# Second attention: key and query slots with four rows per group, returned as one transfer of 128 partitions

## The chip, the core and the metric

The kernel runs on one NeuronCore of a Trainium2 chip. The metric is the device time of one execution in microseconds (us); lower is better. The profile names the engines PE (TensorE), DVE (VectorE), ACT (ScalarE), POOL (GpSimd) and SP (SyncE, which here only issues transfers). SBUF is the on-chip memory of 128 partitions, PSUM holds the results of PE in eight banks.

## The reference, cut to what matters

Four layers over 1024 tokens of 512 numbers, each followed by a residual sum and a layer norm: a small attention across heads, a ternary feed-forward, a windowed causal attention with rotary positions ("the second attention"), and a mixture of experts. The change touches only the second attention:

```python
q = q * cos + rotate_half(q) * sin
k = k * cos + rotate_half(k) * sin
scores = einsum('bhqd,bhkd->bhqk', q, k) / sqrt(16)
allowed = (j <= i) & (j > i - 128)
attn = softmax(where(allowed, scores, -inf))
out = einsum('bhqk,bhkd->bhqd', attn, v) @ Wo.T
```

It has 32 heads of 16 numbers, and each block of 128 query tokens sees its own block of keys and the one before.

## The kernel before, in words

The second attention works on 8 tiles t of 128 tokens. For each tile PE multiplies by the key, query and value weights (`project2`), DVE rotates keys and queries (`rotate`, `rope_sum`), PE turns them so that head dimensions lie along partitions (`turn_rotated`). To keep float32 accuracy from products in a shorter format, each tensor is kept as a high part (ACT, `parts_out_high`) and a low part (DVE, `parts_low`). A product of two such tensors needs three terms: high by high, low by high, high by low.

The three terms are folded into one product by stacking rows. A head has 16 dimensions, and for each of them the stack holds three rows: for keys high, high, low and for queries high, low, high. So a head fills 48 rows. Two heads share the 128 partitions, one from partition 0 and one from partition 64 (`KS` = 64). The stack is built by a detour through device memory (the scratch tensor `ys`, called `slots_out` in the profile):

- SP (`relay_rows`, line 866) writes three blocks of 256 KB for each tensor of each tile. The group of a dimension has 3 rows in device memory, and each write fills one of them.
- POOL (`stack_rows`, line 1803) waits for the three writes and issues two transfers of 384 KB that bring the 96 rows back: 48 rows to partitions 0 to 47, 48 rows to partitions 64 to 111, each row 8 KB. Keys go to `kS` (a part of tile `RP`), four slots in rotation; queries go to `qS` (`XR` or `QS`), three slots in rotation.

Scores are computed twice. `row_scores` (line 573) multiplies queries by keys over 48 rows, and DVE takes the row maxima from it (`row_maxima`, line 1185). The maxima are split, turned, and written by POOL (`stack_maxima`, line 1810, four transfers of 8 KB per tile) as two more rows, 48 and 49 of each half, of `qS`. The matching rows of `kS` hold minus one: POOL sets whole key slots to minus one before first use (`minus_ready`, lines 1792, 1830 and 1838). `key_scores` (line 586) then multiplies keys by queries over 50 rows, which gives scores with the maximum subtracted; ACT exponentiates (`weights_out`), POOL masks (`mask`, lines 1818 and 1821), PE weighs the values (`weigh`, line 601).

One loop, written out by hand in the same form for each engine, sets the order: `for i in range(-1, T)` with eight steps. In turn i the engines do row scores of tile i + 1, key scores of tile i, projections and relay of tile i + 2, and output of tile i - 1. Each engine works through its own list in order. In turn i POOL issues the return of the keys of tile i + 2 in step 4 and of its queries in step 5, then the first maxima of tile i + 1 in step 6. PE needs the returned tile at the first `row_scores` of the next turn, and the maxima at the first `key_scores` behind that. All POOL transfers share one queue (q0). After the last tile's blocks are written, SP issues loads of shared expert weights (768 KB each), a gate matrix and a table.

Of the kernel before, what the change touches and what calls it, by code (L numbers as in the profile page):

```python
# [5 lines left out]
F32 = mybir.dt.float32  # L6
F32R = mybir.dt.float32r
# [8 lines left out]
P = 128  # L16
# [5 lines left out]
HD = D // H  # L22
KS = 64
# [56 lines left out]
def build(nc, x, wq, wk, wv, bias, k0, k1, k2, s0, s1, s2, aq, ak, av, ao, gate, experts, shared,  # L80
          rope_c, factor_c, table_c, out, xs, ys):
    with ExitStack() as ctx:
        def sb(name, shape, dt):
            return ctx.enter_context(nc.sbuf_tensor(name, shape, dt))

        def sem(name):
            return ctx.enter_context(nc.semaphore(name))
# [32 lines left out]
        slots = sb("slots", [P, TOP, T], U32)  # L120
# [5 lines left out]
        with nc.sbuf_tensor("QS", [P, 18432], F32R) as QS:  # L126
# [27 lines left out]
        qS = [t.rearrange("p (a q) -> p a q", q=P) for t in (XR[:, 2048:4096], QS[:, 0:2048], QS[:, 2048:4096])]  # L154
        kS = RP[:, :].rearrange("p (s a k) -> p s a k", s=4, k=P)
# [12 lines left out]
        XT2 = XR[:, 0:2048].rearrange("p (b a c n) -> p b a c n", b=2, a=2, c=DC)  # L168
        x2T = [QS[:, 0:1024].rearrange("p (a c n) -> p a c n", a=2, c=DC)] + [XT2[:, 0]] * (T - 1)
        coT = XT2[:, 1]  # L170
        relay_in = [[ys[a:a + 3 * P, :].bitcast(F32R).rearrange("(d m) n -> d (m n)", m=4) for a in (6 * P * n, 6 * P * n + 3 * P)]
                    for n in range(2)]
        relay = [[ys[a:a + 3 * P, :].rearrange("(x b m) n -> b x m n", b=3, m=4) for a in (6 * P * n, 6 * P * n + 3 * P)]
                 for n in range(2)]

        wblock = [FP[:, c:c + WCOLS] for c in (14336, 14336 + WCOLS, 0, WCOLS, 8704, 8704 + WCOLS)]
        xblock = FP[:, 3072:5120].rearrange("p (b n) -> p b n", b=XB_)
# [85 lines left out]
        parts_out = [sem("qparts_out"), sem("kparts_out")]  # L263
        stack_in = [[sem(f"qstack_in{b}") for b in range(2)], [sem(f"kstack_in{b}") for b in range(2)]]
        max_in = [sem(f"max_in{f}") for f in range(2)]
        minus_ready = sem("minus_ready")
        diag_zero = sem("diag_zero")
        kdiag_in = [sem(f"kdiag_in{n}") for n in range(5)]
        kq_split = sem("kq_split")
# [31 lines left out]
        def window(i):  # L301

            cur, prev = i % 4, (i - 1) % 4
            if i == 0:
                return cur, 0
            if prev < cur:
                return slice(prev, cur + 1, cur - prev), P
            return slice(cur, prev + 1, prev - cur), 0
# [6 lines left out]
        def parts(t, n):  # L315

            return parts_k if n == 1 else parts_q[0 if t < 2 else 1]
# [10 lines left out]
        def _(pe):  # L328
# [171 lines left out]
            def half(hh, rows):  # L500

                return slice(KS * hh, KS * hh + rows)
# [59 lines left out]
            def row_scores(i, s):  # L562

                if s == 0:
                    pe.wait_ge(stack_in[1][i % 2], 32 * (i // 2 + 1))
                    pe.wait_ge(stack_in[0][i % 2], 32 * (i // 2 + 1))
                slots, _ = window(i)
                n = P if i == 0 else 2 * P
                both = [V.fill(pe, ("rowscores", i, 2 * s + a))[:, :].rearrange("p (a k) -> p a k", a=2)[:, :, 0:n] for a in range(2)]
                for m in range(2):  # L570
                    pr = 2 * s + m
                    for a in range(2):
                        mm = nc.tensor.matmul(both[a][:, m, :], qS[i % 3][half(a, 3 * HD), pr, :], kS[half(a, 3 * HD), slots, pr, :],  # L573
                                              start=True, stop=True)
                        if m == 1:
                            mm.then_inc(V.full, 1)

            def key_scores(i, hg, w):

                if w == 0 and hg % 4 == 0:  # L580
                    pe.wait_ge(max_in[hg // 4], 32 * (i + 1))
                both = [Q.fill(pe, ("keyscores", i, hg + a, w)) for a in range(2)]
                for m in range(4):
                    pr = 4 * (hg // 2) + m
                    for a in range(2):
                        mm = nc.tensor.matmul(both[a][:, m * P:(m + 1) * P], kS[half(a, 3 * HD + 2), (i - w) % 4, pr, :],  # L586
                                              qS[i % 3][half(a, 3 * HD + 2), pr, :], start=True, stop=True)
                        if m == 3:
                            mm.then_inc(Q.full, 1)

# [44 lines left out]
            for i in range(-1, T):  # L635
                t, r, d = i + 2, i + 1, i - 1
                for s in range(8):
                    if r < T:
                        row_scores(r, s)
                    if i >= 0 and (s % 2 == 0 or i >= 1):  # L640
                        key_scores(i, 2 * (s // 2), s % 2)
# [63 lines left out]
            b = V.fill(pe, "logits")  # L705
            for t in range(T):
                mm = nc.tensor.transpose(b[:, t * E:(t + 1) * E], lgT[:, t * P:(t + 1) * P], ident[0:E, 0:E])
# [52 lines left out]
            for k in range(len(ITEMS)):  # L760
# [6 lines left out]
                if k == 0:  # L767

                    pe.wait_ge(picked_ready, 2)
                    b = V.fill(pe, "ranks")[:, 0:(T + 1) * E]  # L770
                    nc.tensor.matmul(b, before[:, :], picked[:, :, :], start=True, stop=False)
                    for t in range(T):
                        nc.tensor.matmul(b[:, (t + 1) * E:(T + 1) * E], onesb[:, :], picked[:, t:t + 1, :].broadcast_to([P, T - t, E]),
                                         start=False, stop=False)
# [8 lines left out]
            for t in range(G, T):  # L783
                pe.wait_ge(tile_gathered[t], 16 * TOP)
                pe.wait_ge(diagonals_ready, TOP * G)
                for k in range(TOP):
                    mm = nc.tensor.matmul(acc[t - G][:, :], diagonal[:, TOP * (t - G) + k, :], gathered[:, (TOP * t + k) % YG, :],
                                          start=False, stop=(k == TOP - 1))
# [4 lines left out]
        def _(sp):  # L793
# [29 lines left out]
            def load_raw(n, w):  # L823
                sp.dma_start(raw_c[n].rearrange("p (c n) -> p c n", c=DC), w.rearrange("(c p) n -> p c n", p=P)).then_inc(wc_in[n], 16)
# [3 lines left out]
            for k in range(2 * NCH):  # L828
# [12 lines left out]
                for j in range(G):  # L841
                    rows = slice(32 * j, 32 * j + HD)
# [13 lines left out]
            def relay_rows(t, n):  # L856

                m = 2 * t + 1 - n
                if t >= 2:
                    sp.wait_ge(stack_in[n][t % 2], 32 * (t // 2))  # L860
                for blk, l in ((0, 0), (1 + n, 0), (2 - n, 1)):
                    if l == 0:
                        sp.wait_ge(parts_high, m + 1)
                    else:
                        U.drained(sp, ("turned", t, n))
                    sp.dma_start(relay[n][t % 2][blk], parts(t, n)[:, l, :].bitcast(F32)).then_inc(parts_out[n], 16)

            for t in range(T):
                relay_rows(t, 1)
                relay_rows(t, 0)  # L870
                if t == 1:
                    A.filled(sp, ("hidden", 1, 1, DC - 1))
                    sp.wait_ge(stack_in[0][1], 32)
                    load_raw(3, ao)
            sp.wait_ge(rotated, 2 * T)
            sp.wait_ge(parts_out[0], 48 * T)
# [850 lines left out]
        def _(p):  # L1727
# [14 lines left out]
            for k, (base, step) in enumerate(((0, -1), (-1, 1), (0, -1))):  # L1742
                m = maskb[:, k * P:(k + 1) * P]
# [45 lines left out]
            A.filled(p, ("hidden", 0, 1, DC - 1))  # L1789
            nc.gpsimd.memset(vaug[:, :, :, HD:HD + 1], 1.0).then_inc(ones_ready, 1)  # L1790
            for n in range(2):
                nc.gpsimd.memset(kS[:, n].bitcast(F32), -1.0).then_inc(minus_ready, 1)
            def stack_rows(t, n):

                p.wait_ge(parts_out[n], 48 * (t + 1))
                if t >= 3:
                    Q.filled(p, ("keyscores", t - 3, 7, 1 if t >= 4 else 0))
                if n == 1:
                    p.wait_ge(minus_ready, min(t, 3) + 1)
                rows = relay_in[n][t % 2]  # L1800
                for a in range(2):
                    dst = (qS[t % 3], kS[:, t % 4])[n][KS * a:KS * a + 3 * HD]
                    nc.gpsimd.dma_start(dst.rearrange("d a q -> d (a q)"), rows[3 * HD * a:3 * HD * a + 3 * HD]).then_inc(stack_in[n][t % 2], 16)

            def stack_maxima(t, f):

                U.drained(p, ("mx", t, f))
                for a in range(2):
                    place = KS * a + 3 * HD
                    nc.gpsimd.dma_start(qS[t % 3][place:place + 2, 8 * f:8 * f + 8, :],  # L1810
                                        mxT[HD * a:HD * a + HD, f, :]).then_inc(max_in[f], 16)

            def mask(i, hg, w):
# [10 lines left out]

            stack_rows(0, 1)
            stack_rows(0, 0)
            stack_rows(1, 1)
            stack_rows(1, 0)
            A.filled(p, ("ffn", T - 1))
            nc.gpsimd.memset(kS[:, 2].bitcast(F32), -1.0).then_inc(minus_ready, 1)  # L1830
            for i in range(-1, T):
                t, r = i + 2, i + 1
                for step in range(8):
                    if (i, step) == (1, 0):
                        p.wait_ge(w_high, 16)
                        nc.gpsimd.tensor_tensor(W[:, 7, :], raw_c[3], W[:, 6, :].bitcast(F32), ALU.subtract).then_inc(wo_split, 1)
                    if (i, step) == (0, 3):
                        nc.gpsimd.memset(kS[:, 3].bitcast(F32), -1.0).then_inc(minus_ready, 1)
                    if i >= 0 and (step % 2 == 0 or i >= 1):
                        mask(i, 2 * (step // 2), step % 2)  # L1840
                    if step == 2 and i >= 0:
                        stack_maxima(i, 1)
                    if step == 4 and 2 <= t < T:
                        stack_rows(t, 1)
                    if step == 5 and 2 <= t < T:
                        stack_rows(t, 0)
                    if step == 6 and r < T:
                        stack_maxima(r, 0)
# [76 lines left out]
```

## Time and profile before

| | |
|---|---|
| median of 3 runs | 733.93 us (730.81 to 736.4) |
| profiled execution | 731.17 us |
| its span, first to last instruction | 729.4 us |
| busy: PE / DVE / ACT / POOL | 615.2 / 393.2 / 270.8 / 239.0 us |
| mean granted TensorE clock | 0.918 of 2.4 GHz |
| turns i = 0 to 7 of the second attention | about 250 to 511 us |

Device time is a little longer than the span, since starting and ending the program lie outside it. Busy times overlap; what counts is which engine or transfer the others wait for at a given place. In a row of the timeline the bracket at the end is the idle time of the engine before the row and what released it; "issue" there means that the profile shows no releaser.

### The profile page before, as it was taken

To read this page: it belongs to the slowest core of one execution; us is meant where nothing else is said; L and a number is where in the kernel's file an instruction comes from. 1 tells how busy PE (TensorE), PEld (TensorE's weight loads), DVE (VectorE), ACT (ScalarE), POOL (GpSimd) and SP (SyncE) were. 2 spreads that over 40 slices of the span, in tenths; PEclk is the share of its full clock that TensorE was granted. 3 is DMA by queue.
4 is the path that set the end of the run, shared out by engine and by line. 5 is a ranking of instruction groups with operands and counts; after the bars stand their busy time and mean duration, and the time that the engine had idled before them with its cause. 6 is when DMAs were issued, how large, how long until landed. Compare 5 with 4: busy or idle time off the path is not lost.

```text
span 729.4 us, 13453 instructions
## 1 busy us (share of the span) xinstructions
PE 615.2 (84%) x5108; PEld 485.6 (67%) x5108; DVE 393.2 (54%) x1126; ACT 270.8 (37%) x433; POOL 239.0 (33%) x348
## 2 busy tenths in 40 slices
PE   2998999669889787998979896868789699999985
PEld 2987977557667565666757664645558588888762
DVE  4315445697765775767666684552464133323355
ACT  5155036366563323424243442444530112221313
POOL 6002523543310245535343552462007311111072
PEclk9999999999999886999898997577899899999998
DMA  8921211442057444618171638020007759997455
GB/s 304 392 103 27 54 34 25 104 134 74 0 145 155 106 116 61 155 23 176 35 143 46 131 110 165 2 89 3 0 1 283 279 178 409 415 418 286 185 167 193
DMA packets 49455, 104.37 MB, mean 143 GB/s; under 512 B 12208, under 2 KB 18480, under 8 KB 47856
## 3 DMA queue, kind: packets, MB, share of 16 engines
q1 hardware_dynamic: 30032, 61.68, 24.0%
q0 software_dynamic: 13744, 31.61, 18.9%
q10 hardware_dynamic: 5616, 10.23, 3.9%
q8 instruction: 41, 0.67, 0.4%
q14 instruction: 22, 0.18, 0.1%
HBM read 63.77 MB, written 35.13 MB: 136 GB/s over the span
## 4 chain that ended last, share of the span: by engine, by line
PE 53%; DMA 13%; DVE 10%; ACT 9%; issue 8%; POOL 6%; SPq 1%; POOLq 0%; ACTq 0%; DVEq 0%
PE bank L332 12%; PE bank L515 11%; PE bank L368 9%; DMA slots_out<-FP 5%; ACT FP L1451 4%; DVE FP L915 4%; PE bank L601 3%; PE bank L586 3%; PE bank L573 3%; POOL slots_in L1854 2%; POOL FP L1866 2%; DMA QS<-QS 2%; PE bank L391 2%; PE bank L546 2%; PE bank L379 1%
## 5 line engine op out<-in xcount | busy, mean ns | idle before, releaser
L1451 ACT ACTIVATE FP<-bank 128x512 f32<-128x512 f32 (+1 forms) x244 | 138.7, 611 | 316.3 <-PE bank L586 131.1
L1185 DVE CUSTOM_DVE_ANT_0 kraw<-bank,maskb 128x256 bf16<-128x256 f32 (+1 forms) x256 | 88.5, 401 | 60.1 <-PE bank L573 60.1
L515 PE MATMUL bank<-W,XR 128*128 128x512 f32 x348 | 107.0, 454 | 0.1
L332 PE MATMUL bank<-FP 128*128 128x128 f32 x558 | 89.1, 315 | 1.0 <-ACT FP L1451 1.0
L515 PEld LDWEIGHTS bank<-W,XR 128*128 128x128 f32 x348 | 72.0, 219 | 16.3 <-DVE XR L915 0.3
L368 PE MATMUL bank<-W,XR 128*128 128x512 f32 x288 | 77.6, 419 | 5.2 <-DVE W L915 5.2
L1818 POOL TENSOR_SCALAR_AFFINE_SELECT FP<-FP 128x512 f32<-128x512 f32 x64 | 41.4, 670 | 112.4 <-ACT FP L1451 112.4
L368 PEld LDWEIGHTS bank<-W,XR 128*128 128x128 f32 x288 | 64.2, 271 | 11.8 <-DVE W L915 5.6
L332 PEld LDWEIGHTS bank<-FP 128*128 128x128 f32 x558 | 66.9, 196 | 3.0 <-DVE FP L915 1.6
L915 DVE TENSOR_TENSOR FP<-FP,bank 128x128 f32<-128x128 f32 (+1 forms) x39 | 14.4, 370 | 68.4 <-ACT FP L1451 47.4
L332 PE MATMUL bank<-RP,W 128*128 128x512 f32 x192 | 45.8, 394 | 2.2 <-DVE FP L915 2.2
L1821 POOL TENSOR_SCALAR_AFFINE_SELECT FP<-FP 128x512 f32<-128x512 f32 x56 | 38.0, 705 | 29.3 <-ACT FP L1451 29.1
L1859 POOL DMA_DIRECT2D FP<-slots_in x31 | 16.7, 540 | 86.5 <-PE bank L717 79.9
L1774 POOL DMA_DIRECT2D RPF<-FP x64 | 31.5, 502 | 38.5 <-PE bank L404 27.8
L332 PEld LDWEIGHTS bank<-RP,W 128*128 128x128 f32 x192 | 35.7, 188 | 10.5 <-issue 1.8
L573 PE MATMUL bank<-RP,QS 48*128 48x256 f32 x160 | 23.7, 377 | 22.6 <-issue 11.8
L1386 DVE COPY FP<-bank 128x512 f32<-128x512 f32 x31 | 21.4, 691 | 37.4 <-PE bank L717 37.4
L601 PE MATMUL bank<-FP 128*17 128x128 f32 x960 | 37.9, 308 | 2.0 <-ACT FP L1451 1.8
L915 DVE TENSOR_TENSOR XR<-bank,XR 128x512 fp32r<-128x512 f32 x27 | 21.3, 806 | 31.6 <-ACT XR L1451 31.6
L573 PEld LDWEIGHTS bank<-RP,QS 48*128 48x128 f32 x160 | 14.7, 222 | 34.0 <-issue 24.4
L601 PEld LDWEIGHTS bank<-FP 128*17 128x17 f32 x960 | 26.6, 108 | 13.1 <-issue 6.0
L1854 POOL DMA_INDIRECT slots_in<-X,slots x16 | 16.7, 1045 | 48.1 <-issue 48.1
(168 smaller groups left out, 1019.4 us busy)
## 6 DMA issues: line engine op xcount, KB each, us to landing
FP<-in_experts_dram SPq DMA_DIRECT2D x31, 768.0 KB, 9.6
slots_out<-QS SPq DMA_DIRECT2D x48, 256.0 KB, 2.8
FP<-slots_in POOLq DMA_DIRECT2D x31, 256.0 KB, 6.5
slots_out<-FP ACTq DMA_DIRECT2D x31, 256.0 KB, 8.0
slots_in<-RP SPq DMA_DIRECT2D x7, 1024.0 KB, 13.6
RP<-slots_out POOLq DMA_DIRECT2D x16, 384.0 KB, 6.0
QS<-slots_out POOLq DMA_DIRECT2D x10, 384.0 KB, 8.3
FP<-in_shared_dram SPq DMA_DIRECT2D x4, 768.0 KB, 7.6
```

The lines of the kernel that those rows point to most:

```text
L332: mm = nc.tensor.matmul(bank, lhs, rhs, start=(n == 0), stop=(n == len(terms) - 1))
L368: mm = nc.tensor.matmul(b[:, :], *terms[m], start=(m == 0), stop=(m == 3 * DC - 1))
L515: mm = nc.tensor.matmul(b[:, :], *terms[n], start=(n == 0), stop=(n == len(terms) - 1))
L573: mm = nc.tensor.matmul(both[a][:, m, :], qS[i % 3][half(a, 3 * HD), pr, :], kS[half(a, 3 * HD), slots, pr, :], start=True, stop=True)
L601: mm = nc.tensor.matmul(weighing[32 * q:32 * q + HD + 1, (h // 4 % 4) * P:(h // 4 % 4 + 1) * P], vaug[:, (i - w) % 4, head(h), :], PT[hg % ...
L915: return nc.vector.tensor_tensor(o, a, b, op)
L1185: ins = nc.vector.tensor_tensor_reduce(masked[:, 2 * (f % 2) + m, 0:n], b[:, m, :], maskb[:, m0:m0 + n], 1.0, -BIG, ALU.add, ALU.max, hmax ...
L1451: return nc.scalar.activation(o, i, func, **kw)
L1774: nc.gpsimd.dma_start(vdiag[k % 3][32 * g:32 * g + 32, 272 * g:272 * g + 272].rearrange("p (s d) -> p s d", s=CH), vT[32 * g:32 * g + 32, ...
L1818: ins = nc.gpsimd.affine_select(out=pt, in_=pt, compare_op=ALU.is_ge, fill=0.0, base=0, pattern=[[0, 4], [1, P]], channel_multiplier=-1)
L1821: ins = nc.gpsimd.affine_select(out=pt, in_=pt, compare_op=ALU.is_ge, fill=0.0, base=-1, pattern=[[0, 4], [-1, P]], channel_multiplier=1)
L1854: nc.gpsimd.indirect_dma_start(xs, bass.IndirectOffsetOnAxis(slots[:, k, t:t + 1], 0), X[:, t, :], None).then_inc(scattered, 16)
```

## The change

The group of a dimension has four rows instead of three, in device memory and in SBUF. The fourth row holds minus ones for keys and zeros for queries. These are written once, into both buffers of each tensor, by four transfers of 256 KB that SP issues ahead of the first relay (`edge_in`), from two memsets of 32 partitions (`edge_ready`). A returned tensor is now 128 rows of 8 KB, brought by one transfer to all 128 partitions. The maxima overwrite rows 3 and 7 of each half of the query slot. `row_scores` and `key_scores` run over 64 rows. The memsets of whole key slots, the wait for them in `stack_rows`, and one of the two transfers per tensor are gone; counts of 32 become 16.

```diff
-        relay_in = [[ys[a:a + 3 * P, :].bitcast(F32R).rearrange("(d m) n -> d (m n)", m=4) for a in (6 * P * n, 6 * P * n + 3 * P)]
+        places = [[slice(4 * P * (2 * n + b), 4 * P * (2 * n + b + 1)) for b in range(2)] for n in range(2)]
+        relay_in = [[ys[rows, :].bitcast(F32R).rearrange("(d m) n -> d (m n)", m=4) for rows in of] for of in places]
...
-                        mm = nc.tensor.matmul(both[a][:, m, :], qS[i % 3][half(a, 3 * HD), pr, :], kS[half(a, 3 * HD), slots, pr, :],
+                        mm = nc.tensor.matmul(both[a][:, m, :], qS[i % 3][half(a, KS), pr, :], kS[half(a, KS), slots, pr, :],
...
-                        mm = nc.tensor.matmul(both[a][:, m * P:(m + 1) * P], kS[half(a, 3 * HD + 2), (i - w) % 4, pr, :],
-                                              qS[i % 3][half(a, 3 * HD + 2), pr, :], start=True, stop=True)
+                        mm = nc.tensor.matmul(both[a][:, m * P:(m + 1) * P], kS[half(a, KS), (i - w) % 4, pr, :],
+                                              qS[i % 3][half(a, KS), pr, :], start=True, stop=True)
...
+            for n in range(2):
+                sp.wait_ge(edge_ready, n + 1)
+                for b in range(2):
+                    sp.dma_start(relay[1 - n][b][3].rearrange("x m n -> x (m n)"),
+                                 kS[0:P // 4, n].rearrange("p a k -> p (a k)").bitcast(F32)).then_inc(edge_in, 16)
...
-                nc.gpsimd.memset(kS[:, n].bitcast(F32), -1.0).then_inc(minus_ready, 1)
+                nc.gpsimd.memset(kS[0:P // 4, n].bitcast(F32), (-1.0, 0.0)[n]).then_inc(edge_ready, 1)
...
-                if n == 1:
-                    p.wait_ge(minus_ready, min(t, 3) + 1)
-                rows = relay_in[n][t % 2]
-                for a in range(2):
-                    dst = (qS[t % 3], kS[:, t % 4])[n][KS * a:KS * a + 3 * HD]
-                    nc.gpsimd.dma_start(dst.rearrange("d a q -> d (a q)"), rows[3 * HD * a:3 * HD * a + 3 * HD]).then_inc(stack_in[n][t % 2], 16)
+                if t == 0:
+                    p.wait_ge(edge_in, 64)
+                dst = (qS[t % 3], kS[:, t % 4])[n]
+                nc.gpsimd.dma_start(dst.rearrange("d a q -> d (a q)"), relay_in[n][t % 2]).then_inc(stack_in[n][t % 2], 16)
...
-                    place = KS * a + 3 * HD
-                    nc.gpsimd.dma_start(qS[t % 3][place:place + 2, 8 * f:8 * f + 8, :],
+                    nc.gpsimd.dma_start(qS[t % 3][KS * a + 3:KS * a + 8:4, 8 * f:8 * f + 8, :],
...
-            nc.gpsimd.memset(kS[:, 2].bitcast(F32), -1.0).then_inc(minus_ready, 1)
...
-                    if (i, step) == (0, 3):
-                        nc.gpsimd.memset(kS[:, 3].bitcast(F32), -1.0).then_inc(minus_ready, 1)
```

## Rows read from the trace of the kernel before

**Rows 1.** The page's chain that ended last, shares of the span by engine.

```profile
PE 53%; DMA 13%; DVE 10%; ACT 9%; issue 8%; POOL 6%; SPq 1%; POOLq 0%; ACTq 0%; DVEq 0%
```

**Rows 2.** Windows: length, busy us of five engines, clock share, transfer share, GB/s.

```profile
347.10:380.70 33.60, 29.71 (x300) 22.92 (x300) 22.40 (x91) 12.48 (x23) 14.74 (x24) 0.90 0.45 96
452.90:481.00 28.10, 25.79 (x262) 19.67 (x262) 18.70 (x81) 13.53 (x23) 11.91 (x20) 0.63 0.02 2
```

**Rows 3.** Timeline of PE, first score products of turns 1 to 6.

```profile
281.81 0.80 PE L573 MATMUL bank<-RP,QS 48*128 48x256 f32 x4 [2.86 <-DMA QS<-slots_out]
...
314.11 0.50 PE L573 MATMUL bank<-RP,XR 48*128 48x256 f32 x4 [0.99 <-issue]
315.25 0.66 PE L586 MATMUL bank<-QS,RP 50*128 50x128 f32 x8 [0.64 <-DMA QS<-QS]
...
347.08 0.56 PE L573 MATMUL bank<-RP,QS 48*128 48x256 f32 x4 [2.52 <-issue]
...
380.69 0.50 PE L573 MATMUL bank<-RP,QS 48*128 48x256 f32 x4 [2.36 <-issue]
381.89 0.47 PE L586 MATMUL bank<-QS,RP 50*128 50x128 f32 x2 [0.69 <-DMA QS<-QS]
...
414.91 0.50 PE L573 MATMUL bank<-RP,XR 48*128 48x256 f32 x4 [2.34 <-issue]
...
452.93 0.80 PE L573 MATMUL bank<-RP,QS 48*128 48x256 f32 x4 [6.94 <-issue]
```

**Rows 4.** Timeline of POOL: transfer issues of turn 2, and of turn 5.

```profile
335.27 1.07 POOL L1803 DMA_DIRECT2D RP<-slots_out  x2
...
337.52 1.05 POOL L1803 DMA_DIRECT2D QS<-slots_out  x2
...
435.14 1.07 POOL L1803 DMA_DIRECT2D RP<-slots_out  x2
```

**Rows 5.** Transfer issues within 338.1:338.2 and 341.7:341.8, KB, us to landing.

```profile
QS<-slots_out POOLq DMA_DIRECT2D x1, 384.0 KB, 8.9
...
XR<-QS POOLq DMA_DIRECT2D x1, 8.0 KB, 6.0
```

**Rows 6.** All 32 transfers of line 1810, issue to landing.

```profile
DMA to landing us min/median/max: 1.8/3.1/10.2
```

**Rows 7.** Windows: a return alone; then expert loads. Last column GB/s.

```profile
336.50:345.50 9.00, 8.05 (x136) 5.98 (x134) 6.23 (x27) 3.92 (x8) 5.65 (x10) 1.00 1.15 178
600.00:609.00 9.00, 9.00 (x65) 7.18 (x65) 4.03 (x8) 2.62 (x6) 1.61 (x3) 1.00 1.01 379
```

**Rows 8.** Transfer issues, 430 to 456 us.

```profile
FP<-in_shared_dram SPq DMA_DIRECT2D x2, 768.0 KB, 13.3
...
QS<-slots_out POOLq DMA_DIRECT2D x2, 384.0 KB, 12.9
```

**Rows 9.** Timeline of DVE behind the end of turn 2.

```profile
345.22 0.18 DVE L943 BATCH_NORM_AGGREGATE mv<-st 128x2 f32<-128x6 f32 x1
```

**Rows 10.** Timeline of PE: the two projections of turn 3.

```profile
349.45 5.21 PE L515 MATMUL bank<-W,XR 128*128 128x512 f32 x12
...
355.84 2.99 PE L515 MATMUL bank<-W,XR 128*128 128x512 f32 x12
```

**Rows 11.** Windows of half granted clock in turns 3 and 6.

```profile
347.40:354.20 6.80, 6.80 (x27) 5.47 (x24) 2.21 (x11) 1.09 (x2) 1.22 (x2) 0.50 0.00 0
449.80:473.70 23.90, 18.81 (x158) 14.59 (x160) 12.43 (x59) 9.66 (x15) 8.39 (x14) 0.50 0.12 17
```

**Rows 12.** Instructions by form: weight loads, least, median, longest ns.

```profile
L573 PEld LDWEIGHTS bank<-RP,QS x160: 182/186/335, 250.5 to 475.6; 48*128 48x128 f32 x160
...
L332 PEld LDWEIGHTS bank<-RP,W x192: 186/188/192, 534.5 to 703.4; 128*128 128x128 f32 x192
```

**Rows 13.** Timeline of POOL: the first return, and a memset.

```profile
206.89 1.02 POOL L1803 DMA_DIRECT2D RP<-slots_out  x2 [16.93 <-DMA slots_out<-QS]
...
245.35 1.80 POOL L1830 MEMSET RP<- 128x2048 f32 x1 [5.67 <-PE bank L332]
```

More of the change, by code:

```diff
@@ L170, in build @@
         coT = XT2[:, 1]
-        relay_in = [[ys[a:a + 3 * P, :].bitcast(F32R).rearrange("(d m) n -> d (m n)", m=4) for a in (6 * P * n, 6 * P * n + 3 * P)]
-                    for n in range(2)]
-        relay = [[ys[a:a + 3 * P, :].rearrange("(x b m) n -> b x m n", b=3, m=4) for a in (6 * P * n, 6 * P * n + 3 * P)]
-                 for n in range(2)]
+        places = [[slice(4 * P * (2 * n + b), 4 * P * (2 * n + b + 1)) for b in range(2)] for n in range(2)]
+        relay_in = [[ys[rows, :].bitcast(F32R).rearrange("(d m) n -> d (m n)", m=4) for rows in of] for of in places]
+        relay = [[ys[rows, :].rearrange("(x b m) n -> b x m n", b=4, m=4) for rows in of] for of in places]
         wblock = [FP[:, c:c + WCOLS] for c in (14336, 14336 + WCOLS, 0, WCOLS, 8704, 8704 + WCOLS)]
@@ L265, in build @@
         max_in = [sem(f"max_in{f}") for f in range(2)]
-        minus_ready = sem("minus_ready")
+        edge_ready = sem("edge_ready")
+        edge_in = sem("edge_in")
         diag_zero = sem("diag_zero")
@@ L564, in row_scores @@
                 if s == 0:
-                    pe.wait_ge(stack_in[1][i % 2], 32 * (i // 2 + 1))
-                    pe.wait_ge(stack_in[0][i % 2], 32 * (i // 2 + 1))
+                    pe.wait_ge(stack_in[1][i % 2], 16 * (i // 2 + 1))
+                    pe.wait_ge(stack_in[0][i % 2], 16 * (i // 2 + 1))
                 slots, _ = window(i)
@@ L859, in relay_rows @@
                 if t >= 2:
-                    sp.wait_ge(stack_in[n][t % 2], 32 * (t // 2))
+                    sp.wait_ge(stack_in[n][t % 2], 16 * (t // 2))
                 for blk, l in ((0, 0), (1 + n, 0), (2 - n, 1)):
@@ L872, in _ @@
                     A.filled(sp, ("hidden", 1, 1, DC - 1))
-                    sp.wait_ge(stack_in[0][1], 32)
+                    sp.wait_ge(stack_in[0][1], 16)
                     load_raw(3, ao)
```

## The prediction

> **What bounds the kernel now.** I read the views in this order: the page's chain, the second attention cut into its turns, the waits of PE at the turn boundaries, the transfers that end those waits, and the clock.
>
> The chain is PE for 53% of the span and transfers for 13% [rows 1]; some of its "issue" share is transfers too, as will be seen. In a middle turn PE is busy 29.71 of 33.60 us, DVE 22.40, POOL 14.74, ACT 12.48 [rows 2]. PE is the bound there, so a microsecond in which PE stands still in a turn is one lost, and the other engines have room. The long stops of PE all sit at the same place, the first row scores of a new turn: 2.86, 0.99, 2.52, 2.36, 2.34 and 6.94 us in turns 1 to 6, and twice the first key scores behind them, 0.64 and 0.69 us [rows 3]. Together 19.34 us.
>
> Who ends them? In turn 1 the profile names the returned queries, elsewhere it says "issue". The landings settle it. For the tile that turn 3 needs, POOL issues the keys from 335.27 and the queries from 337.52 [rows 4]. The second half of the queries, issued near 338.1, takes 8.9 us, so it lands at 347.0; PE starts at 347.08 [rows 3, 5]. The first maxima stand behind it on POOL's queue: near 341.7 they need 6.0 us, where the quickest of that line needs 1.8 [rows 5, 6]. So the return ends the wait at each boundary, and it delays the maxima as well.
>
> **Part 1: the return is one transfer of 128 partitions.** The fixed part of a POOL transfer I take as 1.8 us, the quickest landing of an 8 KB one [rows 6]. From the issue of the keys to the landing of the queries are 11.7 us (335.27 to 347.0), of which 9.9 us carry four times 384 KB, 1.57 MB: 159 GB/s. A window laid over it shows 178 GB/s with the transfer engines busy throughout (share over 1), while expert loads to all 128 partitions, with stores and other loads beside them, run at 379 GB/s with a share of 1.01 [rows 7]. So the engines here are not short of work but slow at it: each transfer writes into only 48 partitions.
>
> The new return brings 2.10 MB in two transfers. At 379 GB/s that is 5.5 us; with 1.8 us it lands at 342.6, at 159 GB/s it is 13.2 us and lands at 350.3. These are the ends. I take 379, because the width of the destination is what sets the two rows apart. PE is free at 344.56 (347.08 less 2.52). Any rate above 2.10 MB in 7.5 us, 280 GB/s, hides the return wholly; below 212 GB/s (2.10 MB in 9.9 us) it is later than now.
>
> The Trainium skill, "SBUF — State Buffer", section "Door 1: The DMA port swizzle", says that a transfer's rate follows from how many of 16 ports its partitions reach, that partitions 0 to 63 reach only 8, and that two transfers on the two halves, issued together, hardly gain on one. The rows with 48 partitions agree in direction. By its 328 GB/s for 1 MiB on 128 partitions, an estimate, the return would land at 343.5, still hidden.
>
> What is late next at a boundary? DVE's last work of turn 2 ends at 345.40, 0.84 us after PE is free [rows 9], but that is the layer norm's statistics; PE's two banks for row scores were emptied before it. The maxima, issued near 341.7 behind the queries, land by 343.5 with 1.8 us. So in turns 2 to 5 I count the stops wholly: 0.99 + 0.64 + 2.52 + 2.36 + 0.69 + 2.34 = 9.54 us. In turn 1 the last return issue is later against PE, and 2.86 us are gained if it is 2.86 us earlier; 4.4 us (9.9 less 5.5) are at hand, so 2.86.
>
> Turn 6 is different: the shared loads of 1.57 MB run beside the return, both land after about 13 us [rows 8]. Return and shared loads are 3.67 MB; at 379 GB/s from the keys' issue at 435.14 [rows 4], with 1.8 us, all is in at 446.6, where PE is free at 445.99 [rows 3]. The keys are ahead of the shared loads, the queries among them. I take a rest of 0.9 us, with ends of 0 and 3, so 6.0 us are gained. Sum of part 1: 9.54 + 2.86 + 6.0 = 18.4 us.
>
> **Part 2: the clock.** Behind a stop at a boundary PE often runs at half clock. In turn 3 the granted clock is 0.50 from 347.4 to 354.2 [rows 11], that is 1.2 of 2.4 GHz, after the idle 2.52 us; twelve products take 5.21 us in it and 2.99 us after it [rows 10]. So a half-clocked us of PE work gives back 1 - 2.99/5.21 = 0.43 us. Like stretches follow the other stops in turns 2 to 5, at most 6.8 us each. Three times 6.8 us, 20.4 us, would give 8.8 us as an upper end; the lower end is 0, since a fall can also have another cause. I take 5 us. Turn 6 runs at half clock until 473.7 [rows 11], 20.8 us of it, which would be 8.9 us; but the turn has few large products, and DVE with 18.70 us of work in 28.10 [rows 2] soon becomes the bound. I take 1 us there and 1 us in turn 1, ends 0 and 6. Sum: 7 us.
>
> The stops could go without their clock; then the gain is 18.4 us alone.
>
> **Part 3: longer products.** Four products of 256 columns over 48 rows take 0.50 us [rows 3], that is 1024 columns; twelve of 512 over 128 rows take 2.99 us, which is also 0.50 us for 1024 [rows 10]. Weight loads take 186 ns at 48 rows and 188 at 128 [rows 12]. Rows are free; 0.
>
> **Part 4: the edge rows.** Two memsets stay, with fewer partitions; two of 1.80 us go, one of them ahead of the first maxima of turn 0, where PE next waits for DVE, so 0 gained [rows 13]. SP issues four more transfers of 256 KB while it would wait anyway: the first return waits 16.93 us for its blocks and is issued at 206.89 [rows 13], and is needed over 20 us later. Cost 0; if that cover were gone, four issues and the transfers, some 5 us. The added wait for `edge_in` stands ahead of the first return only, where nothing else is queued that PE needs.
>
> **Part 5: one POOL issue less per tensor.** Half of 1.07 us each [rows 4] falls away. The queries are issued about 0.5 us sooner; this is margin, 0.
>
> **Sum.** 18.4 + 7 = 25.4 us. The profiled execution took 731.17 us, so 705.8; it lay 2.8 us under the median 733.93. Against the median: 708.5, said as 708.
>
> **Rivals.**
>
> A, the price goes by bytes (slower). If the return is slow for another reason than the 48 partitions, say reads of scratch rows in device memory, 2.10 MB at 159 GB/s need 13.2 us instead of 9.9: 3.3 us more at each of six boundaries, 20 us, and the clock stays as it is: 754. The place is PE's wait at each turn's first row scores, and it decides from 212 GB/s down. For it: POOL's queue shows no fast large transfer alone in these rows. Against: 379 GB/s with POOL's own block loads in it [rows 7]. The Trainium skill, "DMA: Bandwidth & Descriptors", section "Anatomy of one DMA", has a fit by bytes alone, 2.0 us plus bytes over 436 GB/s: an estimate of 2.9 us for 384 KB and 4.4 us for 1 MB, one transfer for two of which would gain next to nothing. Its 2.9 us stand against 8.9 us in the trace.
>
> B, stops go, another wait comes. The rotation on DVE, the exponentials on ACT or the maxima's way become late once PE is ahead, and the clock still falls, as half clock is also seen where PE never waited for a return. Then half to two thirds of 18.4 us are gained: 9 to 12, which gives 722 to 725.
>
> C, nothing measurable: the stop is ended by something that only coincides with the landing. Then 734. The landing at 347.0 and the start at 347.08 speak against it.
>
> **How the numbers follow.** Forecast, stops gone and part of the clock back: 0.75, 700 to 717. B: 0.13. A: 0.05. C: 0.03. More than that, with turn 6 at full clock (19.3 + 8.8 + 7 = 35, so 699 or less): 0.04. The upper end of the range takes in part of B, stops gone by two thirds and no clock: 722. The lower end is 698. No change is within 1% (7 us), about what a measurement here can tell; A is the slower case, with a little for a clock that gets worse: faster 0.91, same 0.04, slower 0.05.
>
> **What would show it.** Right: returned tensors of 1 MB land within 5 to 6 us of issue; the stops of PE at the first row scores are under 0.5 us in turns 1 to 5 and under 3 in turn 6; the maxima land in about 2 us; a middle turn lasts 28 to 31 us instead of 33.6. Wrong: landings of 7 us or more, rate in the return under 212 GB/s; or fast landings with new idle time of PE before turned or weighed tiles; or half-clock stretches that stay though the stops are gone.

## The result and the profile after

The changed kernel takes 707.76 us (median of 4 runs, 702.0 to 710.99) against 732.37 us before (4 runs): a ratio of 0.9649 with a 95% interval of 0.9569 to 0.973. The profiled execution took 710.99 us, its span is 709.3 us, at a mean granted clock of 0.926. It is the slowest of the four runs, so its span tells a little less than the medians: 20.1 us less than before, where the medians differ by 24.6.

The page's chain, to set beside [rows 1]: transfers fall from 13% to 6%, PE rises from 53% to 60%.

```profile
PE 60%; DVE 11%; ACT 9%; issue 6%; DMA 6%; POOL 5%; SPq 1%; POOLq 0%; ACTq 0%; DVEq 0%
```

The timeline of PE at the same first products as [rows 3]; a turn without a bracket began without a stop:

```profile
279.78 0.80 PE L573 MATMUL bank<-RP,QS 64*128 64x256 f32 x4 [0.75 <-DVE hmax L1190]
...
309.83 0.50 PE L573 MATMUL bank<-RP,XR 64*128 64x256 f32 x4 [0.58 <-issue]
311.40 0.66 PE L586 MATMUL bank<-QS,RP 64*128 64x128 f32 x8 [1.06 <-DMA QS<-QS]
...
340.53 0.50 PE L573 MATMUL bank<-RP,QS 64*128 64x256 f32 x4
...
368.86 0.51 PE L573 MATMUL bank<-RP,QS 64*128 64x256 f32 x4 [0.41 <-issue]
...
396.76 0.50 PE L573 MATMUL bank<-RP,XR 64*128 64x256 f32 x4
...
427.30 0.80 PE L573 MATMUL bank<-RP,QS 64*128 64x256 f32 x4 [2.62 <-issue]
428.83 1.11 PE L586 MATMUL bank<-XR,RP 64*128 64x128 f32 x8 [0.73 <-DMA XR<-QS]
```

The stops add up to 6.15 us where there were 19.34. Ahead of turns 3 and 5 there is none. Turn 0 now ends on the row maxima of DVE, a new releaser in place of the returned queries, and over half of what is left (2.62 and 0.73 us) stands before turn 6, where the shared loads run beside the return.

The transfer that stood at 335.27 and 337.52 before is issued at 329.78 and 331.90 now. Each is one transfer; size in KB and us from issue to landing (windows 329.9:330 and 332.1:332.2):

```profile
RP<-slots_out POOLq DMA_DIRECT2D x1, 1024.0 KB, 5.3
```

```profile
QS<-slots_out POOLq DMA_DIRECT2D x1, 1024.0 KB, 7.0
```

So the queries land at 338.9, 9.1 us after the keys' issue (11.7 before), and PE comes for them at 340.53: 1.6 us of margin.

Windows: the first two answer to [rows 2], the middle one to the return in [rows 7], the last two to [rows 11].

```profile
340.50:368.90 28.40, 26.44 (x304) 20.51 (x300) 22.71 (x93) 12.89 (x24) 13.76 (x22) 1.00 0.39 133
427.30:455.70 28.40, 25.52 (x252) 19.24 (x252) 17.48 (x79) 12.32 (x20) 11.90 (x20) 0.59 0.02 4
...
331.00:338.60 7.60, 7.60 (x75) 5.18 (x73) 3.51 (x18) 3.29 (x7) 4.17 (x8) 0.78 0.83 279
...
426.50:450.40 23.90, 20.40 (x167) 15.63 (x167) 13.21 (x64) 9.65 (x15) 8.39 (x14) 0.50 0.04 10
460.60:484.50 23.90, 20.80 (x167) 14.49 (x168) 3.52 (x10) 8.77 (x15) 9.60 (x17) 0.50 0.15 53
```

Turn 3 lasts 28.4 us, 5.2 less than before, at full clock throughout. The window begins behind the stop ahead of turn 3, so of these 5.2 us only 2.0 are a stop, the one at its end ahead of turn 4 (2.36 us, now 0.41). The rest is work: PE is busy for 26.44 us in it where it needed 29.71, with the same products, at the other clock. Turn 6 is the exception. It is 28.4 us long and was 26.7 (452.93 to the first product of turn 7 at 479.63), and about 23 us of it, from its start to 450.4, are at half clock.

### The profile page after: what moved, and what is told of

Same layout as the page of the kernel before. It is cut to its first block, busy times and chain, and to the rows that moved or that the text cites. A ratio compares the mean times of both kernels' runs of the same rounds, so it can differ in the third digit from the quotient of the medians.

```text
span 709.3 us, 13439 instructions
## 1 busy us (share of the span) xinstructions
PE 607.8 (86%) x5108; PEld 479.8 (68%) x5108; DVE 393.1 (55%) x1126; ACT 270.8 (38%) x433; POOL 228.3 (32%) x330
## 3 DMA queue, kind: packets, MB, share of 16 engines
q1 hardware_dynamic: 30224, 62.73, 24.6%
## 4 chain that ended last, share of the span: by engine, by line
PE 60%; DVE 11%; ACT 9%; issue 6%; DMA 6%; POOL 5%; SPq 1%; POOLq 0%; ACTq 0%; DVEq 0%
PE bank L332 17%; PE bank L515 11%; PE bank L368 9%; ACT FP L1456 4%; DVE FP L920 4%; PE bank L601 4%; PE bank L586 3%; PE bank L573 3%; POOL slots_in L1853 2%; PE bank L717 2%; POOL FP L1865 2%; DVE kraw L1190 2%; PE bank L391 2%; PE bank L379 1%; PE bank L546 1%
## 5 line engine op out<-in xcount | busy, mean ns | idle before, releaser
L515 PE MATMUL bank<-W,XR 128*128 128x512 f32 x348 | 99.8, 429 | 0.1
L368 PE MATMUL bank<-W,XR 128*128 128x512 f32 x288 | 76.3, 414 | 5.2 <-DVE W L920 5.2
L515 PEld LDWEIGHTS bank<-W,XR 128*128 128x128 f32 x348 | 66.5, 202 | 14.6 <-DVE XR L920 0.3
L368 PEld LDWEIGHTS bank<-W,XR 128*128 128x128 f32 x288 | 63.6, 270 | 11.1 <-DVE W L920 5.6
L1823 POOL TENSOR_SCALAR_AFFINE_SELECT FP<-FP 128x512 f32<-128x512 f32 x56 | 37.9, 701 | 23.6 <-ACT FP L1456 23.3
L920 DVE TENSOR_TENSOR XR<-bank,XR 128x512 fp32r<-128x512 f32 x27 | 21.3, 807 | 31.9 <-ACT XR L1456 31.9
L601 PEld LDWEIGHTS bank<-FP 128*17 128x17 f32 x960 | 26.6, 108 | 13.2 <-issue 5.7
L573 PE MATMUL bank<-RP,QS 64*128 64x256 f32 x160 | 23.7, 378 | 11.5 <-DVE hmax L1190 8.5
L717 PEld LDWEIGHTS bank<-ident,FP 128*128 128x128 f32 x124 | 15.7, 144 | 21.5 <-issue 15.7
```

The source lines that it names most:

```text
L368: mm = nc.tensor.matmul(b[:, :], *terms[m], start=(m == 0), stop=(m == 3 * DC - 1))
L515: mm = nc.tensor.matmul(b[:, :], *terms[n], start=(n == 0), stop=(n == len(terms) - 1))
L573: mm = nc.tensor.matmul(both[a][:, m, :], qS[i % 3][half(a, KS), pr, :], kS[half(a, KS), slots, pr, :], start=True, stop=True)
L601: mm = nc.tensor.matmul(weighing[32 * q:32 * q + HD + 1, (h // 4 % 4) * P:(h // 4 % 4 + 1) * P], vaug[:, (i - w) % 4, head(h), :], PT[hg % ...
L920: return nc.vector.tensor_tensor(o, a, b, op)
L1823: ins = nc.gpsimd.affine_select(out=pt, in_=pt, compare_op=ALU.is_ge, fill=0.0, base=-1, pattern=[[0, 4], [-1, P]], channel_multiplier=1)
```

## Experiments

The kernel before was timed again beside each group of kernels: median 734.0 us beside two halves, two combs, the later loads in the changed kernel and the first kernel with idle products in turn 6; 729.9 us beside the others. So kernels of different groups are compared by their ratios to the kernel before, not by their medians.

**Two halves, and two combs.** Both keep the four-row layout, its bytes and the new loads of 64 rows; only the return is cut in two.

```diff
-                nc.gpsimd.dma_start(dst.rearrange("d a q -> d (a q)"), relay_in[n][t % 2]).then_inc(stack_in[n][t % 2], 16)
+                for a in range(2):
+                    nc.gpsimd.dma_start(dst[KS * a:KS * a + KS].rearrange("d a q -> d (a q)"), relay_in[n][t % 2][KS * a:KS * a + KS])\
+                        .then_inc(stack_in[n][t % 2], 16)
```

The combs differ in the slices alone: `dst[a:P:2]` and `relay_in[n][t % 2][a:P:2]`.

> The changed kernel, but each tensor returns in two transfers of 512 KB, one to partitions 0 to 63 and one to partitions 64 to 127; same bytes, same rows, same products. Theory (the rate follows from how widely one transfer spreads over the partitions): the return is slow again. Before, 1.57 MB in four such transfers took 9.9 us behind a fixed 1.8 us; now 2.10 MB take between 9.9 and 13.2 us, so keys' issue to queries' landing is 11.7 to 15 us against 9.1 us in the changed kernel, the stops of PE at the first row scores come back with 2.5 to 5 us each, and the time is 728 to 752 us. Rival (one transfer fewer per tensor is what helps, or bytes alone count): one more issue of 0.53 us per tensor and nothing else, 707 to 713 us.

> The changed kernel, but each tensor returns in two transfers of 512 KB, one to the even and one to the odd partitions. Theory (spread over the partitions): both transfers reach as far as one of 128 partitions, so the return takes 9 to 10 us as in the changed kernel, and the time is 705 to 713 us. Rival (the single transfer is what helps): as slow as with two halves, 728 us or more. Neither kernel changes the number of bytes.

Measured: two halves 735.95 us (10 runs), a ratio of 1.0069 to the kernel before (1.0024 to 1.0114); two combs 704.52 us (4 runs), 0.9666 (0.9596 to 0.9735). Windows over one return, first of the kernel with halves, then of the one with combs (last column GB/s):

```profile
340.00:350.00 10.00, 9.56 (x136) 6.74 (x134) 5.81 (x26) 3.64 (x8) 5.60 (x10) 0.83 1.10 210
```

```profile
331.30:338.00 6.70, 6.70 (x96) 5.09 (x98) 4.16 (x21) 3.32 (x7) 5.52 (x10) 1.00 0.95 318
```

Issue to landing of all their returns of line 1807, halves and then combs:

```profile
DMA to landing us min/median/max: 4.9/7.3/15.6
```

```profile
DMA to landing us min/median/max: 3.8/4.9/10.3
```

From the issue of turn 3's keys to the landing of its queries are 12.9 us with halves (338.73 to 351.60) and 8.6 with combs (330.08 to 338.70). The transfer engines are about as busy in the one as in the other (1.10 and 0.95) and move 210 and 318 GB/s. Same bytes, same number of transfers, same queue: what differs is which partitions one transfer reaches. With halves the stops are back (4.30, 2.90, 2.13, 3.84, 3.32 and 9.20 us before turns 1 to 6), and the layout with more bytes is a small loss, 0.2 to 1.1%. This settles the spread of a transfer against rival A (bytes) and against "one transfer instead of two": the single transfer is not what helps. One thing moves along with the partitions: row d of the scratch tensor always goes to partition d, so a comb also reads every other row of device memory and a half reads adjacent ones. No run parts the two; that it is the side of the partitions is argued, not shown. The Trainium skill, "SBUF — State Buffer", section "Door 1: The DMA port swizzle", gives partition bits 2 to 4 and 6 as the choice of port; even and odd partitions alone reach every port by it. The combs agree, at 318 GB/s against 210. The same page says that only one transfer over all 128 partitions can reach all of them ("Can I just issue two DMAs to hit both halves?"); two combs of 64 partitions, which bring a tensor pair back as fast as two transfers over all 128 or faster (8.6 us against 9.1), are against that sentence.

**Stops filled with idle products, in the kernel before.** The products are extra work and change no result.

```diff
+                    if s == 0 and 1 <= i <= 6:
+                        fill_in((0, 12, 4, 10, 9, 9, 28)[i])     # products of 512 columns into a free bank
```

> The kernel before, with its slow return, but with idle products of 512 columns on PE ahead of the first row scores of turns 1 to 6 (12, 4, 10, 9, 9 and 28 of them), about as long as the stops of PE there and no longer. The stops keep their length but PE is busy in them. This measures the clock's part alone. Theory (the half-clock stretches behind the stops come from the stops): the stretches near 316, 347, 381, 415 and 450 us go, and 5 to 12 us are gained with no transfer made faster: 722 to 729 us. Rival (the stretches fall by chance or for other reasons): they stay and the time is 733 to 740 us.

Measured: 725.52 us (10 runs), 0.9952 of the kernel before (0.991 to 0.9995). Its timeline of PE ahead of turn 3, and the windows of turns 2 and 3:

```profile
344.76 2.25 PE L639 MATMUL bank<-W 128*128 128x512 f32 x9
347.86 0.51 PE L573 MATMUL bank<-RP,QS 48*128 48x256 f32 x4 [0.85 <-issue]
```

```profile
316.10:347.90 31.80, 29.16 (x310) 22.32 (x310) 22.40 (x91) 12.49 (x23) 14.74 (x24) 1.00 0.50 102
347.90:379.80 31.90, 28.88 (x309) 22.11 (x309) 22.39 (x91) 12.48 (x23) 14.73 (x24) 1.00 0.50 101
```

The trace has nine of the ten products issued there. PE comes to the row scores about as late as before, but works while it waits, and turns 2 and 3 stay at 2.4 GHz; turn 3 takes 31.9 us instead of 33.6. Turns 2 to 5 together take 131.9 us instead of 138.8. So the clock is a second price of a stop, and it is separable: 6.9 us in this profile for turns 2 to 5. Not all reaches the end: the twelve products ahead of turn 1 outlast the stop (turn 0 and its end take 33.9 us instead of 31.3). Turn 6 is still at half clock for 17.1 us, though 6.65 us of products stand in its stop and only 1.19 and 0.33 us of idle time are left:

```profile
451.40:468.50 17.10, 15.13 (x136) 11.45 (x136) 9.69 (x47) 8.57 (x13) 7.24 (x13) 0.50 0.02 3
```

The interval leaves 0.4 to 6.6 us for the whole, under 1%, where 5 to 12 was expected; the stretches behind the stops go as the theory said, up to turn 5, but the time gained, 3.5 us by the ratio, is less.

**Shared loads issued after the last return.** In the changed kernel, and in the kernel before.

```diff
             sp.wait_ge(parts_out[0], 48 * T)
+            sp.wait_ge(stack_in[0][1], 16 * (T // 2))            # 32 in the kernel before
             load_shared(0)
```

> The changed kernel, but SP waits for the landing of the last returned queries before it issues the first load of shared expert weights. Theory (the rest of the stop before turn 6, 2.62 and 0.73 us, comes from the shared loads on the same transfer engines): the queries land 7 us after issue instead of 9.7, the stop before turn 6 falls under 0.8 us, and 2.5 to 3.4 us are gained; the shared weights land about 6 us later and ACT needs the first of them some 6 us into turn 6, so 0 to 3 us of this may be lost. If the clock of turn 6 hangs on that stop, the half-clock stretch from 426 to 450 us goes too, for up to 6 us more: 699 to 706 us. Rival (the clock of turn 6 is low because the turn has few large products): the stop goes but the stretch stays, 704 to 708 us.

> The kernel before, but SP waits for the landing of the last returned queries before it issues the first load of shared expert weights. In the kernel before those loads land about 13 us after issue together with the queries. Theory (the stop of 6.94 us before turn 6 is the slow return plus the collision): the queries land 8 to 9 us after issue instead of 13, the stop before turn 6 becomes 2 to 3 us, and 4 to 5 us are gained, 728 to 731 us. Rival (the stop is the narrow return alone): no gain, 733 us.

Measured: 699.11 us (4 runs), 0.9593 of the kernel before (0.9522 to 0.9665); in the kernel before 726.99 us (10 runs), 0.9971 (0.9927 to 1.0016), which is not told from no change. Transfers of the first of these, 411 to 440 us, and its timeline and window at the start and over the length of turn 6:

```profile
FP<-in_shared_dram SPq DMA_DIRECT2D x2, 768.0 KB, 5.0
QS<-slots_out POOLq DMA_DIRECT2D x1, 1024.0 KB, 7.1
```

```profile
423.70 0.50 PE L573 MATMUL bank<-RP,QS 64*128 64x256 f32 x4
```

```profile
423.70:447.00 23.30, 19.38 (x254) 14.87 (x252) 17.78 (x81) 13.01 (x21) 11.91 (x20) 0.85 0.24 79
```

The queries land 7.1 us after issue where they took 9.7 beside the loads, and turn 6 starts without a stop. The loads themselves land in 5.0 us instead of 10.6 (medians of two), so waiting costs them little: they are in at 427.9 and 429.95 us, where the changed kernel had them at 425.5 and 428.4. Turn 6 then takes 23.3 us at a mean clock of 0.85 instead of 28.4 at 0.59. My rival, that the half-clock stretch stays when the stop goes, falls: it shrinks from 23.9 to 6.8 us. But the stop is not the whole cause. The 6.8 us that stay begin at 429.8, 6 us into a turn that began without a stop, and in the kernel before with filled stops turn 6 was at half clock for 17.1 us. What else lowers the clock in this turn is not shown. In the kernel before, the same wait cuts the stop ahead of turn 6 from 6.94 to 2.06 us, as expected, but turn 6 still begins with a stop and is at half clock for 17 us; the 4 to 5 us that this should have gained are not told from nothing in the time.

By its ratio the changed kernel with the later loads is the fastest that ran, level with the two kernels built on it below. Its four runs, 698.1 to 700.54 us, all lie below the changed kernel's four, 702.0 to 710.99; by the ratios, 0.9593 and 0.9649, the gain over the changed kernel is 4 us, by the medians 8.7, and the intervals of the ratios overlap. The gain is seen in the trace, in the stop and in turn 6; its size is open.

**Idle products in turns 6 and 7.** In the changed kernel (8 and then 3 per step of turn 6), and with the later loads (2 per step of turn 6, 4 of turn 7).

```diff
+                    if i in (6,) and s < 5:
+                        fill_in(8 if s == 0 else 3)
```

> The changed kernel with idle products on PE: 8 products of 512 columns ahead of the first row scores of turn 6 and 3 more ahead of each of its steps 1 to 4, 20 in all, from weights into a bank that nobody reads before it is overwritten. They add about 20 x 0.23 = 4.6 us of PE work at 2.4 GHz or 8 at 1.2 GHz; the first eight fall into the stop of 2.6 us. Theory (turns with few large products run at half clock, and PE is their bound only for that reason): the granted clock stays 1 through most of turn 6, its 28.4 us become 24 to 27, and the time is 703 to 708 us. Rival (the clock doesn't follow from PE's work here, or DVE and ACT bound the turn anyway): the turn grows by 2 to 6 us, 709 to 714 us.

> The changed kernel with the shared loads issued after the last return, and with idle products on PE: 2 of 512 columns ahead of each of the first five steps of turn 6, 4 ahead of each of the first five of turn 7. If a busy PE holds the full clock where nothing else is wrong, turns 6 and 7 run mostly at 2.4 GHz and up to 5 us are gained on the 699 us of the kernel with the later loads: 694 to 700 us. If turn 7 is bound by the chain through ACT, POOL and PE in turn, not by PE's clock, it is 699 to 703 us.

Measured: 704.67 us, 0.9655 (0.9581 to 0.9728), and 699.39 us, 0.9602 (0.9554 to 0.965). The window of turn 6 in the first:

```profile
426.30:454.30 28.00, 23.29 (x275) 16.50 (x274) 19.23 (x81) 13.79 (x23) 12.14 (x21) 0.94 0.05 8
```

The clock does follow PE's work: 0.94 instead of 0.59, and the turn (426.33 to 452.65) takes 26.3 us instead of 28.4. Against the changed kernel the time is no different within the intervals, and with the stop gone the idle products buy nothing: 699.39 us at a mean clock of 0.949 to 0.958 against 699.11 us at 0.941. It looks as if what they return in clock they take as work.

**Both helpful edits together.**

> The changed kernel with both edits that helped: the shared loads issued after the last return, and each tensor returned in two transfers, to the even and to the odd partitions. If the combs' queries, landing 5.5 us after their issue instead of 7, only add margin where PE no longer waits, 697 to 701 us, as with the later loads alone. If the quicker return helps turns 1 and 6 or the maxima as well, 694 to 697 us.

Measured: 699.94 us, 0.961 (0.9561 to 0.9658), as with the later loads alone. Once the return lands before PE comes, a quicker one (queries in 5.7 us instead of 7.0, medians of the profiles) is only margin.

## Why the prediction was right

Forecast 708 us in 698 to 722; measured 707.76. The mechanism held: the return was slow because each transfer reached few partitions, and with it went most of the stops and much of the half clock. That the time comes out within 1 us is partly luck. The forecast gain was 25.4 us; the medians differ by 24.6, but the profiled executions, where the terms can be counted, by 20.1 only. Of the terms the stops and turns 6 and 7 came out under the forecast, the clock ahead of turn 6 above it, and these cancelled in part.

- **The stops end with the return** held: with the return quicker they went, with halves they came back, at unchanged products. "Wholly" did not hold: of the stops in turns 1 to 5, 2.80 us are left.
- **Width sets the rate** held in the sense of spread over the partitions, with the reservation given at the combs. The size was off: I took 379 GB/s and a landing 7.3 us after the keys' issue; the window has 279 GB/s and 9.1 us. This was almost at the threshold of 280 GB/s that I had worked out for wholly hiding the return, and it explains why 0.58 and 0.41 us are left ahead of turns 2 and 4, where the queries landed 9.8 and 9.6 us after the keys' issue, 0.09 us ahead of PE's first product. From 331 to 334 us the return does run at 330 GB/s, and then falls off as the engines' share falls from 1.03 to 0.55 (336 to 338.5 us, 206 GB/s). By the 328 GB/s of the Trainium skill, "SBUF — State Buffer", section "Door 1: The DMA port swizzle", an estimate of the landing is 8.2 us: nearer to the 9.1 measured, but still short.
- **Stops gained**: 18.4 us forecast, 13.2 measured (19.34 less 6.15). Of turn 1's 2.86 us only 2.11 went: DVE's row maxima were next, which the forecast did not have there. Before turn 2 nothing went: 1.64 us against 1.63, first the queries, landing 7.7 us after issue, then the maxima. In the kernels with combs or later loads it is under 0.9 us, so its length in this one profile is partly chance. Before turn 6, 3.35 us stayed; I had taken 0.9 within 0 to 3. The "about 13 us" that I read for return and shared loads together were medians of two each: the loads landed 10.7 and 15.9 us after issue, the queries 10.8 and 14.9.
- **The clock**: 5 us forecast in turns 2 to 5. Half-clocked time there fell from 23.9 us to 3.4 us; at my 0.43 that is 8.8 us, the upper end that I had written down, and filling the stops alone showed 6.9 us. In turns 0 and 1 it fell from 20.5 to 13.7 us, which at 0.43 is 2.9 us where I had taken 1. The doubt (falls with another cause) was right for a small part: the stretch from 436.1 to 439.5 us before lies in the middle of turn 5, and the 3.4 us that are left (330.9 to 334.3) in the middle of turn 2, both behind no stop at a boundary. Mostly it was too cautious: in all six kernels whose return was quick (the changed one, the combs, the later loads and the three built on them) the half-clocked time there is 0 to 3.4 us.
- **Turns 6 and 7**: a gain of 1 us forecast for turn 6; measured a loss of 1.7 us in turn 6 and 3.0 us in turn 7 (479.63 to the next layer's first product at 512.46, now 455.66 to 491.49). The half-clocked stretch of turn 7 is 23.9 us now and was 17.1. For turn 6 the later loads show that most of the half-clocked stretch hangs on the stop ahead of it, and that full clock there is worth about 4 us (28.4 to 23.3, less the 0.73 us of the second wait), not the 1 us that I had taken because DVE would soon be the bound. The loss of 1.7 us adds up: the half-clocked stretch is 23.9 us long in both kernels, but with the shorter stop less of it lies in the stop and 23.1 us instead of 20.8 in the turn, at 0.43 1.0 us; the other 0.73 us is the wait at the first key scores, which had none before. For turn 7 it stays open: the later loads and the combs have 13.7 to 17.1 us there, and no run isolated it; the changed kernel's other three runs are up to 9 us quicker at a clock of 0.935 to 0.937, so part of it is the draw of this execution.
- **Longer products free**: held, 0.50 us for four products of 256 columns at 64 rows as at 48. **Edge rows free**: the four extra stores were issued in 2.72 us from 188.09, while the first blocks went out at 202.63:

```profile
188.09 2.72 SPq L871 DMA_DIRECT2D slots_out<-RP  x4
202.63 1.90 SPq L866 DMA_DIRECT2D slots_out<-QS  x3
```

Of the signs that I had set, a middle turn of 28 to 31 us held (28.4), and so did a stop under 3 us before turn 6 by its row scores (2.62). Stops under 0.5 us held before turns 3, 4 and 5, not before turns 1 and 2 (0.75 and 0.58). The landings missed: the keys took 5.0 to 7.1 us and the queries 6.1 to 9.7, and "landings of 7 us or more" stood among the signs of being wrong. That sign was set too tight: queries queue behind their keys, and in turn 3 they hid behind PE with 7.0 us.

Summed over the profile: at the first product of turn 6 the changed kernel is 25.6 us ahead (452.93 less 427.30). The stops up to there stand for 13.9 us of it (19.34 less 5.42), and the 27.3 us less at half clock, at 0.43, for the other 11.7. Turns 6 and 7 then give back 4.7 us, what follows 0.9 more, and 20.1 us are left, by which the span fell.

## What to carry to other kernels

Look at how many partitions one transfer reaches, and which, before its bytes: 33% more bytes over all 128 partitions came back sooner (9.1 us after the first issue against 11.7) than fewer bytes in transfers of 48 partitions, and interleaved partitions serve as well as one full transfer. A stop of PE can cost more than its length, because the products behind it may run at half clock; here filling the stops with work, at their full length, gave back 6.9 us in turns 2 to 5. And once a return is hidden, look for what else shares its transfer engines: one wait that moved four loads behind it took away the last long stop and shortened the turn behind it by 5 us, for about 4 us in the time by the ratios, with intervals that overlap.

## What the runs showed of the hardware

- Two transfers per tensor of 64 adjacent partitions move 210 GB/s with the transfer engines fully busy (share 1.10), two of 64 alternate ones 318 GB/s (0.95); one of 128 partitions starts at 330 and means 279 over the whole return. The rows read in device memory alternate with the partitions.
- PE kept busy with products that nobody needs holds 2.4 GHz through a wait of some 3 us (clock 1.00 in turns 2 and 3, where it fell to 0.50 for 6.8 us behind the idle stop ahead of turn 3).
- A stop ahead of a turn with few large products can have a long tail: around 3.35 us of stops turn 6 of the changed kernel had 23.9 us at half clock, without the stop 6.8 us. Filling it is not always enough: with 6.65 us of idle products in the stop and 1.52 us of idle time left, the kernel before had 17.1 us.
- A short stop need not lower the clock: in the kernel before with later loads PE stood for 1.43 us ahead of turn 3 (349.45 us), and the clock stayed at 2.4 GHz until 369.1 us.
